# Causal masks of a four-layer transformer kernel moved wholly into PSUM, as 64x64 matmuls

## The chip, the cores and the metric

The kernel runs on one core of one Trainium2 chip. The metric is the device time of one execution in microseconds (us); three runs of the kernel before gave 1212.94 to 1221.29 us, median 1218.53.

## What is computed

Four layers, one after the other, on x of 4 sequences x 256 tokens x 512 features. Each layer normalises the rows, computes an attention s and a feed-forward g of the same normalised rows, and adds their product:

```python
xn = _layernorm(x, axis=-1)
s = _L0_attn_ref(xn, L0_attn_Wq, L0_attn_Wk, L0_attn_Wv, L0_attn_Wo)
g = _silu(_L0_ffn_ref(xn, L0_ffn_w_gate, L0_ffn_w_up, L0_ffn_w_down))
x = x + s * g
```

The attention of layers 0, 2 and 3 has 32 query heads and 8 key heads of 16 features, rotary positions and a causal mask (a key behind the query gets no weight); that of layer 1 has 32 key heads and neither. The causal part:

```python
scores = jnp.einsum('bhqd,bhkd->bhqk', q, k)
causal = jnp.triu(jnp.ones((S, S), dtype=bool), k=1)
scores = jnp.where(causal[None, None], -jnp.inf, scores)
attn = jax.nn.softmax(scores / jnp.sqrt(jnp.float32(hd)), axis=-1)
```

The feed-forward parts differ (ternary octonion weights, 4-bit weights, block-scaled weights, low-rank weights); the change leaves them alone.

## The kernel before

**Units and groups.** A layer's attention is worked in 8 units (a sequence and one half of its heads, 16 query heads), each in 4 groups of 4 heads; two layers make a run (r = 0: layers 0 and 1; r = 1: layers 2 and 3) of 16 units and 64 groups, numbered G. Each engine has its own program, written out by hand, and all go through the same slots: `slot(r, G)` is one group's turn on each engine. Between the runs stand the feed-forward parts of layers 0 and 2 (ffn0, ffn2), at the end that of layer 3; layer 1's and parts of the others fill slots.

**Stacks.** To get close to fp32 from fast matmuls, each head's query and key are split into a high and a low part. The parts stand side by side in a stack of 64 columns: 48 (STACK) carry data, column 48 is the place for the row's maximum (the key side holds 1 there), and columns 49 to 63 are zero. `set_pads(l)` and `set_key_pads(l)` on GpSimd fill these columns, once ahead of layer 0 (in ffn0) and once ahead of layer 2 (in ffn2). TensorE turns the stacks (L829, L843), two heads at a time, so that heads lie in partitions 0 to 63 and 64 to 127; a matmul over 64 partitions then gives scores, and two such matmuls use the two halves of the array's rows.

**Two kinds of scores.** `scores_rows` (L863; queries in partitions) serves only to find each query's maximum: VectorE reduces it (L1906), TensorE turns the maxima (L880), and SP copies them by DMA into row 48 of the turned queries (`place_maxima`). `scores_cols` (L905 for the causal layers; keys in partitions) computes the scores again with the maximum already subtracted, for two blocks of keys: kb = 1 (128 queries) and kb = 0 (256 queries). ScalarE takes the exponential of each (L1446) into `probs`, and `weigh_values` (L925) multiplies them with the values, four heads at once in four column tiles of the array (128*32), one slot later.

**The mask before.** For the row scores TensorE adds it in PSUM: for each of the two query blocks qb, four bf16 matmuls of 64 rows by 128 columns (L872), `cut_rows` against `cut_keys`. For the probabilities GpSimd sets the future to zero with `affine_select` (`cut_future`, L2139), two per group, at the head of its slot and ahead of the rest of its queue (`context_low`, `stack_low`, `scale_context`); `weigh_values` waits for them on `causal_cut`.

**The order of TensorE's slot.** `scores_cols(kb=1)` of group G; `scores_rows` qb = 0 and qb = 1 of group G + LEAD (five ahead); `scores_cols(kb=0)` of G; then, by slot, the turning of stacks, a projection (L812), parts of a feed-forward (L679, L712), the weighing of values of G - 1, an output projection (L950). The last five slots of layer 0 compute row scores of layer 1, which have no mask, and the last five of layer 3 none. The row scores of the first five groups of layers 0 and 2 are issued in ffn0 and ffn2, where a block of them stands between matmuls over the whole array.

**Constants.** SP loads 8 constants (CONSTS); VectorE copies the two of the mask into bf16 at step e = 2 of ffn0.

## Time and profile before

| what | value |
|---|---|
| three runs, median | 1218.53 us (1212.94 to 1221.29) |
| the profiled execution, its own time | 1219.86 us |
| its span, first to last instruction | 1218.1 us |
| mean granted TensorE clock | 0.986 of full speed |
| TensorE (PE) / its weight loads (PEld) | 94% / 69% of the span |
| VectorE (DVE) / ScalarE (ACT) / GpSimd (POOL) | 63% / 54% / 41% |
| causal slots, layer 0 | about 169 to 340 us |
| causal slots, layers 2 and 3 | about 835 to 1157 us |

Times in the trace are us from the start of the span. Matmuls are pipelined: a row's length reaches to its modelled end and overlaps the next, so the pace of TensorE is read from start to start. "64\*128" behind an operation is the part of the array that it uses, contraction rows by output columns; "128x512" is partitions by elements. A bracket at the end is the idle time ahead of it and what ended it; "issue" means that nothing the profile shows was waited for.

### The profile page before, as it was taken

To read this page: it belongs to the slowest core of one execution; us is meant where nothing else is said; L and a number is where in the kernel's file an instruction comes from. 1 tells how busy PE (TensorE), PEld (TensorE's weight loads), DVE (VectorE), ACT (ScalarE), POOL (GpSimd) and SP (SyncE) were. 2 spreads that over 40 slices of the span, in tenths; PEclk is the share of its full clock that TensorE was granted. 3 is DMA by queue.
4 is the path that set the end of the run, shared out by engine and by line. 5 is a ranking of instruction groups with operands and counts; after the bars stand their busy time and mean duration, and the time that the engine had idled before them with its cause. 6 is when DMAs were issued, how large, how long until landed. Compare 5 with 4: busy or idle time off the path is not lost.

```text
span 1218.1 us, 22076 instructions
## 1 busy us (share of the span) xinstructions
PE 1144.7 (94%) x8476; PEld 843.3 (69%) x8476; DVE 772.1 (63%) x1124; ACT 655.0 (54%) x1199; POOL 502.0 (41%) x648
## 2 busy tenths in 40 slices
PE   5999999999999999989999999999899999998997
PEld 4788876776656565556687888777677767676665
DVE  7843457785865746684644465545788777775545
ACT  4434347675555655564332333325867676776654
POOL 0000026564422212124555544432775566646552
PEclk8999989999999999999999999999999999999999
DMA  7000010030000100001243222210100101010001
GB/s 277 1 1 1 1 36 2 2 116 2 2 1 2 40 1 1 27 28 53 78 132 102 91 91 78 78 61 5 51 3 2 44 2 34 5 40 12 2 2 69
DMA packets 15258, 48.04 MB, mean 39 GB/s; under 512 B 2858, under 2 KB 6959, under 8 KB 14388
## 3 DMA queue, kind: packets, MB, share of 16 engines
q1 hardware_dynamic: 15156, 46.63, 11.4%
q8 instruction: 70, 1.15, 0.4%
q14 instruction: 32, 0.26, 0.1%
HBM read 44.00 MB, written 2.10 MB: 38 GB/s over the span
## 4 chain that ended last, share of the span: by engine, by line
PE 74%; DVE 12%; ACT 7%; issue 4%; DMA 2%; POOL 1%; DVEq 0%; ACTq 0%; SPq 0%; POOLq 0%
PE bank L679 18%; PE bank L812 16%; PE bank L712 9%; PE bank L950 8%; PE bank L925 6%; PE bank L863 4%; DVE negmax L1906 4%; PE bank L905 4%; ACT probs L1446 3%; DMA W_lo_whole<-in_w 2%; PE bank L872 2%; PE bank L829 1%; PE bank L630 1%; DVE W_lo_whole L1676 1%; ACT qT L1418 1%
## 5 line engine op out<-in xcount | busy, mean ns | idle before, releaser
L1906 DVE TENSOR_REDUCE negmax<-bank 128x4 f32<-128x1024 f32 (+1 forms) x256 | 250.5, 1017 | 100.1 <-PE bank L872 80.2
L1446 ACT ACTIVATE probs<-bank 128x512 f32<-128x512 f32 (+1 forms) x224 | 188.2, 847 | 52.4 <-PE bank L905 51.0
L2139 POOL TENSOR_SCALAR_AFFINE_SELECT probs<-probs 128x512 f32<-128x512 f32 x192 | 123.3, 648 | 169.1 <-ACT probs L1446 167.7
L2061 POOL TENSOR_TENSOR W_lo<-W_lo_whole,W_hi 128x512 fp32r<-128x512 f32 x84 | 117.3, 1425 | 100.0 <-ACT W_hi L1175 100.0
L925 PE MATMUL bank<-probs,V 128*32 128x256 f32 (+1 forms) x2048 | 117.3, 347 | 8.2 <-ACT probs L1446 4.5
L1175 ACT ACTIVATE W_hi<-W_lo_whole 128x1536 fp32r<-128x1536 f32 x28 | 41.7, 1489 | 130.7 <-DVE W_lo_whole L1676 130.7
L863 PE MATMUL bank<-kT,qT 64*128 64x256 f32 (+1 forms) x1024 | 102.6, 296 | 9.7 <-DVE xT_lo L1557 3.5
L905 PE MATMUL bank<-qT,kT 64*128 64x256 f32 (+1 forms) x512 | 97.2, 395 | 11.0 <-ACT qT L1418 4.1
L1457 ACT ACTIVATE pv<-bank 128x256 f32<-128x256 f32 x128 | 49.8, 389 | 97.7 <-PE bank L925 97.7
L925 PEld LDWEIGHTS bank<-probs,V 128*32 128x32 f32 x2048 | 53.6, 109 | 63.9 <-issue 28.5
L863 PEld LDWEIGHTS bank<-kT,qT 64*128 64x128 f32 x1024 | 79.0, 188 | 22.8 <-issue 7.7
L679 PE MATMUL bank<-xT_hi,W_hi 128*128 128x512 f32 x224 | 90.3, 403 | 4.1 <-ACT silu L1188 2.7
L812 PE MATMUL bank<-Wqkv,xT_whole 128*128 128x512 f32 (+1 forms) x256 | 87.9, 497 | 0.9
L1200 ACT ACTIVATE h_hi<-h_lo_whole 128x512 fp32r<-128x512 f32 x72 | 45.5, 633 | 80.2 <-DVE h_lo_whole L1688 52.2
L679 PE MATMUL bank<-xT_hi,W_lo 128*128 128x512 f32 x224 | 87.6, 391 | 0.0
L679 PE MATMUL bank<-xT_lo,W_hi 128*128 128x512 f32 x224 | 87.5, 391 | 0.0
L812 PEld LDWEIGHTS bank<-Wqkv,xT_whole 128*128 128x128 f32 x256 | 47.8, 192 | 38.0 <-issue 35.0
L1676 DVE TENSOR_TENSOR W_lo_whole<-W_lo_whole,block_scales 128x1536 f32<-128x1536 f32 x28 | 50.3, 1796 | 35.4 <-DMA W_lo_whole<-in_w 35.4
L1418 ACT ACTIVATE qT<-bank 128x512 fp32r<-128x512 f32 x128 | 69.4, 601 | 4.9 <-PE bank L829 4.9
L812 PE MATMUL bank<-Wqkv_hi,xT_hi 128*128 128x384 f32 x192 | 69.5, 362 | 2.6 <-ACT probs L1446 1.9
L905 PEld LDWEIGHTS bank<-qT,kT 64*128 64x128 f32 x512 | 48.1, 189 | 32.6 <-issue 23.3
L2108 POOL TENSOR_TENSOR scaled<-pvT,recip 128x256 f32<-128x256 f32 x64 | 43.1, 673 | 63.4 <-DVE recip L1937 63.4
(214 smaller groups left out, 2668.1 us busy)
## 6 DMA issues: line engine op xcount, KB each, us to landing
W_lo_whole<-in_w SPq DMA_DIRECT2D x28, 768.0 KB, 4.2
Wqkv_lo_whole<-in_Wqkv SPq DMA_DIRECT2D x6, 768.0 KB, 6.9
Wo_lo_whole<-in_Wo SPq DMA_DIRECT2D x4, 1024.0 KB, 5.3
Wqkv<-in_Wqkv SPq DMA_DIRECT2D x2, 1536.0 KB, 7.9
Wdown_whole<-in_Wd SPq DMA_DIRECT2D x1, 2816.0 KB, 14.6
x<-in_x SPq DMA_DIRECT2D x4, 512.0 KB, 6.4
out<-x SPq DMA_DIRECT2D x8, 256.0 KB, 2.0
V_lo_whole<-in_V SPq DMA_DIRECT2D x1, 1408.0 KB, 6.2
```

The costliest lines, as they stand in the source:

```text
L679: ins = mm(ps[:], lh, rh, start=(c == 0), stop=(c == len(terms) - 1))
L712: ins = mm(B.tensor(key), lh, rh, start=(j == 0 and c == 0), stop=(j == C - 1 and c == len(terms) - 1))
L812: ins = mm(ps[:, 0:width], lh, rh, start=(c == 0), stop=(c == len(terms) - 1))
L863: ins = mm(ps[:, par, pl * nk:(pl + 1) * nk], A[l].qT[u % 2][half, 2 * g + pl, qb * P:(qb + 1) * P], A[l].kT[u % 2][half, key_slot(l, g, p ...
L905: ins = mm(ps[:, par, pairs[0] * nq:pairs[1] * nq].rearrange("p (h q) -> p h q", h=n), A[l].kT[u % 2][r, key_slot(l, g, pairs[0]), kb * P: ...
L925: ins = mm(ps[32 * i:32 * i + 32, q0:SEQ], A[l].Vflat[u % 4][:, (kb * A[l].vh + kv) * CELL:(kb * A[l].vh + kv) * CELL + 32], A[l].probs[gi ...
L950: ins = mm(ps[:], lh, rh, start=(c == 0), stop=(c == len(terms) - 1))
L1418: nc.scalar.activation(A[l].qT[u % 2][:, 4 * half:4 * half + 4, tau * P:(tau + 1) * P], B.tensor(key).rearrange("p (a t) -> p a t", a=4), ...
L1446: nc.scalar.activation(A[l].probs[gi % 2][kb][:, :, q0 - kb * A[l].probs1:].rearrange("p (b h) q -> p b h q", b=2), B.tensor(key)[:, :, 0: ...
L1906: v.tensor_reduce(A[l].negmax[u % 2][:, qb, :].rearrange("p (b h) -> p b h", b=2)[:, :, 2 * g:2 * g + 2], B.tensor(key)[:, :, 0:2 * nk].re ...
L2061: ins = gp.tensor_tensor(lo, whole, hi.bitcast(F32), ALU.subtract)
L2139: gp.affine_select(out=blk, in_=blk, compare_op=ALU.is_ge, fill=0.0, base=0, pattern=[[0, 4], [1, P]], channel_multiplier=-1).then_inc(cau ...
```

## The change

- In the key stacks, one of the zero columns holds −2^100 for the keys in the second half (64 to 127) of a 128-token block, and in the query stacks the same column holds 1 for the queries in the first half; there is one such column per block (49 for the first, 50 for the second). The score matmuls of both kinds so add −2^100 to a whole 64x64 block of each diagonal 128x128 block, with no instruction of its own. `set_pads` writes these columns: 7 more instructions each for layers 0 and 2.
- What is left of the mask are the triangles of the two 64x64 blocks on the diagonal. For the row scores there are four matmuls per block as before, now of 64 rows by 64 columns, with the output on 64 partitions.
- The column scores get the same: four matmuls of 64 rows by 64 columns behind each of kb = 1 and kb = 0, ahead of the exponential.
- `cut_future` on GpSimd and the semaphore `causal_cut` are gone; `weigh_values` waits for the exponential of kb = 0.
- `cut_rows` and `cut_keys` become one constant `cuts` (128 x 5 x 64) and a second, `half_marks` (128 x 2). NEG is −2^100 instead of −1e30. GpSimd waits for the constants ahead of `set_pads(0)`.

```diff
--- before.py
+++ after.py
@@ -50,7 +50,7 @@
 STACK = 3 * SPLIT
 CELL = HD + 4
 RING = 6
-NEG = -1.0e30
+NEG = -2.0 ** 100
 ROUND = 1.5 * 2.0 ** 23
 WIDTH0 = 1366 // 8
 HID0, HC0 = 8 * WIDTH0, 11
@@ -269,8 +269,8 @@
         xn = [nc.alloc_sbuf_tensor_at(f"xn{i}", [P, D], F32, offset=names["gate"][0] + i * D * 4) for i in range(TILES)]
         ident = place("ident", [P, P], F32)
         ident_r = place("ident_r", [P, P], F32R)
-        cut_rows = place("cut_rows", [P, 2, P], BF16)
-        cut_keys = place("cut_keys", [P, 2, 2, 64], BF16)
+        cuts = place("cuts", [P, 5, 64], BF16)
+        half_marks = place("half_marks", [P, 2], F32)
         cosT = {l: place(f"cos{l}", [P, 2, HD], F32) for l in (0, 2, 3)}
         sinT = {l: place(f"sin{l}", [P, 2, HD], F32) for l in (0, 2, 3)}
         stats = place("stats", [P, TILES, 6], F32)
@@ -405,8 +405,7 @@
         assert at[0] <= R + first["V"] and R + first["negmax"] <= hidden_from
         at = [WP]
         ones = place("ones", [P, P], F32, at)
-        cut_rows_f = place("cut_rows_f", [P, 2, P], F32, at)
-        cut_keys_f = place("cut_keys_f", [P, 2, 2, 64], F32, at)
+        cuts_f = place("cuts_f", [P, 5, 64], F32, at)
         sign_in = place("sign_in", [P, KC, OCT], F32, at)
         sign_hid = place("sign_hid", [P, HC0, OCT], F32, at)
         compact0 = [nc.alloc_sbuf_tensor_at(f"compact{m}", [P, OCT, WIDTH0], F32, offset=WA + m * QKV_BYTES // 2)
@@ -515,7 +514,7 @@
             return Mark(nc, ctx, name, per_layer)
 
         ones_set = mark("ones_set", [3, 0, 0, 0])
-        mask_set = mark("mask_set", [3, 0, 0, 0])
+        mask_set = mark("mask_set", [2, 0, 0, 0])
         ln_stat = mark("row_stats", [TILES] * 4)
         ln_mom = mark("row_moments", [TILES] * 4)
         ln_var = mark("row_variance", [SEQS] * 4)
@@ -563,9 +562,8 @@
         HI = 2
         stack_hi = mark("stack_hi", [16 * HI] * 4)
         stack_lo = mark("stack_lo", [32] * 4)
-        PADS = [6 + 4 * 4, 4, 6 + 3 * 4, 0]
+        PADS = [6 + 7 + 4 * 4, 4, 6 + 7 + 3 * 4, 0]
         pads = mark("pads_set", PADS)
-        causal_cut = mark("causal_cut", [64, 0, 64, 64])
         rs_ready = mark("reciprocal_ready", [4 * SEQS] * 4)
         x_done = mark("x_updated", [TILES] * 4)
 
@@ -792,7 +790,7 @@
                     else:
                         pe.wait_ge(qkv_in[l][u], 16)
                 if u == 0 and tau == 0:
-                    pe.wait_ge(*mask_set.at(0, 3))
+                    pe.wait_ge(*mask_set.at(0, 2))
                 pe.wait_ge(*B.emptied(("xT", l, t)))
                 for key, c0, width in ([(("qkv", l, u, tau), 0, 384)] if GQA[l] else
                                        [(("qkv", l, u, tau), 0, 512), (("v", l, u, tau), 512, 256)]):
@@ -867,9 +865,9 @@
                     for j in range(2):
                         for par in range(2):
                             half = slice(64 * par, 64 * par + 64)
+                            dst = ps[64 * j:64 * j + 64, par, 0:2 * nk].rearrange("p (h k) -> p h k", h=2)
                             k0 = nk - P + 64 * j
-                            dst = ps[:, par, 0:2 * nk].rearrange("p (h k) -> p h k", h=2)[:, :, k0:k0 + 64]
-                            ins = mm(dst, cut_rows[half, j, :], cut_keys[half, j, :, :], start=False, stop=(j == 1))
+                            ins = mm(dst[:, :, k0:k0 + 64], cuts[half, 0, :], cuts[half, 1:3, :], start=False, stop=True)
                 ins.then_inc(B.fills(key), 1)
 
             def turn_max(l, u, bank=None):
@@ -904,7 +902,13 @@
                         r = slice(64 * par, 64 * par + 64)
                         ins = mm(ps[:, par, pairs[0] * nq:pairs[1] * nq].rearrange("p (h q) -> p h q", h=n),
                                  A[l].kT[u % 2][r, key_slot(l, g, pairs[0]), kb * P:(kb + 1) * P],
-                                 A[l].qT[u % 2][r, 2 * g + pairs[0]:2 * g + pairs[1], q0:SEQ], start=True, stop=True)
+                                 A[l].qT[u % 2][r, 2 * g + pairs[0]:2 * g + pairs[1], q0:SEQ], start=True, stop=not CAUSAL[l])
+                if CAUSAL[l]:
+                    for j in range(2):
+                        for par in range(2):
+                            r = slice(64 * par, 64 * par + 64)
+                            dst = ps[64 * j:64 * j + 64, par, 0:2 * nq].rearrange("p (h q) -> p h q", h=2)
+                            ins = mm(dst[:, :, 64 * j:64 * j + 64], cuts[r, 0, :], cuts[r, 3:5, :], start=False, stop=True)
                 ins.then_inc(B.fills(key), 1)
 
             def weigh_values(r, G, slot):
@@ -912,10 +916,7 @@
                 u, g = divmod(gi, GROUPS)
                 key = ("PV", l, gi)
                 ps = claim(key, values_bank(*divmod(slot, GROUPS)))
-                if CAUSAL[l]:
-                    pe.wait_ge(*causal_cut.at(l, 2 * (gi + 1)))
-                else:
-                    pe.wait_ge(*B.emptied(("ST", l, u, g, 0)))
+                pe.wait_ge(*B.emptied(("ST", l, u, g, 0)))
                 for tau in range(2):
                     pe.wait_ge(*B.emptied(("qkv" if GQA[l] else "v", l, u, tau)))
                 for kb in range(2):
@@ -1766,8 +1767,7 @@
                         scale_rows(0, LATE_ROWS[e + 1][0] // 2)
                     if e == 2:
                         dve.wait_ge(const_in, 16 * CONSTS)
-                        v.tensor_copy(cut_rows[:], cut_rows_f[:]).then_inc(mask_set.sem, 1)
-                        v.tensor_copy(cut_keys[:], cut_keys_f[:]).then_inc(mask_set.sem, 1)
+                        v.tensor_copy(cuts[:], cuts_f[:]).then_inc(mask_set.sem, 1)
                     if e + 2 < HC0 + LAG[0]:
                         ternary(after_step[e + 1], after_step[e + 2])
                     hidden(0, e)
@@ -2084,13 +2084,26 @@
 
             def set_key_pads(l):
                 for i in range(2):
-                    gp.memset(A[l].kstack[i][:, :, :, STACK:STACK + 1].bitcast(F32), 1.0).then_inc(pads.sem, 1)
-                    gp.memset(A[l].kstack[i][:, :, :, STACK + 1:64].bitcast(F32), 0.0).then_inc(pads.sem, 1)
+                    kr = A[l].kstack[i][:].rearrange("p n h s -> p (n h) s")
+                    ks = kr.bitcast(F32)
+                    gp.memset(ks[:, :, STACK:STACK + 1], 1.0).then_inc(pads.sem, 1)
+                    c = STACK + 1
+                    if CAUSAL[l]:
+                        if i == 1:
+                            gp.memset(ks[:, :, c:c + 1], 0.0).then_inc(pads.sem, 1)
+                        c += i
+                        gp.tensor_copy(kr[:, :, c], half_marks[:, 1:2].to_broadcast([P, 2 * A[l].kn])).then_inc(pads.sem, 1)
+                        c += 1
+                    gp.memset(ks[:, :, c:64], 0.0).then_inc(pads.sem, 1)
 
             def set_pads(l):
 
                 for i in range(2):
-                    gp.memset(A[l].qstack[i][:, :, STACK:64].bitcast(F32), 0.0).then_inc(pads.sem, 1)
+                    qs = A[l].qstack[i][:].bitcast(F32)
+                    c = STACK + 1 + i
+                    gp.memset(qs[:, :, STACK:c], 0.0).then_inc(pads.sem, 1)
+                    gp.tensor_copy(A[l].qstack[i][:, :, c], half_marks[:, 0:1].to_broadcast([P, UH])).then_inc(pads.sem, 1)
+                    gp.memset(qs[:, :, c + 1:64], 0.0).then_inc(pads.sem, 1)
                 set_key_pads(l)
                 for i in range(4):
                     gp.memset(A[l + 1].V[i][:, :, :, HD:HD + 1], 1.0).then_inc(pads.sem, 1)
@@ -2129,21 +2142,8 @@
                 gp.tensor_tensor(ks[:, :, 32:48], src[:, UH:UH + n, :], ks.bitcast(F32)[:, :, 0:16],
                                  ALU.subtract).then_inc(stack_lo.sem, 1)
 
-            def cut_future(r, G):
-                l, gi = group(r, G)
-                u, g = divmod(gi, GROUPS)
-                for kb in (1, 0):
-                    pool.wait_ge(*B.emptied(("ST", l, u, g, kb)))
-                    q0 = kb * (P - A[l].probs1)
-                    blk = A[l].probs[gi % 2][kb][:, :, q0:q0 + P]
-                    gp.affine_select(out=blk, in_=blk, compare_op=ALU.is_ge, fill=0.0, base=0,
-                                     pattern=[[0, 4], [1, P]], channel_multiplier=-1).then_inc(causal_cut.sem, 1)
-
             def slot(r, G):
                 U, g = divmod(G, GROUPS)
-                l, u = unit(r, U)
-                if CAUSAL[l]:
-                    cut_future(r, G)
                 if pair_turned(G - 1) is not None:
                     context_low(r, pair_turned(G - 1))
                 if r == 0 and (U, g) == (6, 0):
@@ -2216,6 +2216,7 @@
             for b in range(2, SEQS):
                 inverse_deviation(0, b)
             pool.wait_ge(*B.filled(("up", 0, 1, 4)))
+            pool.wait_ge(const_in, 16 * CONSTS)
             set_pads(0)
             for u in range(2):
                 for tau in range(2):
@@ -2246,7 +2247,7 @@
                 load(x[:, 2 * b:2 * b + 2, :], xv[:, 2 * b:2 * b + 2, :], x_in[b])
             load(W0_whole[2][:], a["Wd0"], ffn_in[2])
             n = 0
-            for dst, name in [(cut_rows_f, "cut_rows"), (cut_keys_f, "cut_keys")] + [(cosT[l], f"cos{l}") for l in (0, 2, 3)] + \
+            for dst, name in [(cuts_f, "cuts"), (half_marks, "half_marks")] + [(cosT[l], f"cos{l}") for l in (0, 2, 3)] + \
                     [(sinT[l], f"sin{l}") for l in (0, 2, 3)]:
                 load(dst[:], a[name], const_in)
                 n += 1
@@ -2356,15 +2357,13 @@
     eye = np.eye(P, dtype=np.float32)
     o["ident"] = eye
     r = np.arange(64)
-    rows = np.zeros((64, 2, P), np.float32)
-    rows[r, 0, r] = 1
-    rows[r[:63], 1, 64 + r[:63]] = 1
-    rows[63, 1, 0:64] = 1
-    keys = np.zeros((64, 2, 2, 64), np.float32)
-    keys[:] = np.where(r[None, :] > r[:, None], np.float32(NEG), np.float32(0))[:, None, None, :]
-    keys[63, 1] = NEG
-    o["cut_rows"] = np.concatenate([rows, rows])
-    o["cut_keys"] = np.concatenate([keys, keys])
+    cuts = np.zeros((64, 5, 64), np.float32)
+    cuts[r, 0, r] = 1
+    cuts[:, 1:3] = np.where(r[None, :] > r[:, None], np.float32(NEG), np.float32(0))[:, None, :]
+    cuts[:, 3:5] = np.where(r[None, :] < r[:, None], np.float32(NEG), np.float32(0))[:, None, :]
+    second = np.arange(P) >= 64
+    o["half_marks"] = np.stack([np.where(second, 0.0, 1.0), np.where(second, NEG, 0.0)], 1).astype(np.float32)
+    o["cuts"] = np.concatenate([cuts, cuts])
     which, sign = octonion_table()
     i_of = np.arange(D) // 64
     o["sign_in"] = np.ascontiguousarray(sign[i_of].reshape(KC, P, OCT).transpose(1, 0, 2))
```

## Rows read from the trace of the kernel before

**Rows 1.** The page: busy time by engine.

```profile
PE 1144.7 (94%) x8476; PEld 843.3 (69%) x8476; DVE 772.1 (63%) x1124; ACT 655.0 (54%) x1199; POOL 502.0 (41%) x648
```

**Rows 2.** Stretches: length, then busy of PE, PEld, DVE, ACT, POOL; granted clock.

```profile
170.00:330.00 160.00, 154.01 (x1478) 110.26 (x1482) 115.42 (x180) 106.08 (x214) 88.64 (x134) 0.97 0.07 24
...
815.00:1000.00 185.00, 173.71 (x1773) 132.94 (x1772) 134.91 (x214) 125.56 (x260) 103.98 (x148) 0.99 0.07 23
1000.00:1165.00 165.00, 153.81 (x1495) 111.30 (x1494) 112.12 (x176) 115.39 (x226) 102.63 (x138) 0.99 0.05 17
```

**Rows 3.** The page: shares of the chain that ended last, by engine.

```profile
PE 74%; DVE 12%; ACT 7%; issue 4%; DMA 2%; POOL 1%; DVEq 0%; ACTq 0%; SPq 0%; POOLq 0%
```

**Rows 4.** TensorE groups by form: busy, mean ns | idle before, its releaser.

```profile
L925 PE MATMUL bank<-probs,V 128*32 128x256 f32 x1280 | 96.2, 391 | 8.2 <-ACT probs L1446 4.5 <-DVE negmax L1906 3.5
...
L872 PE MATMUL bank<-cut_keys,cut_rows 64*128 64x128 bf16 x768 | 57.8, 224 | 0.0
```

**Rows 5.** Timeline, one causal slot, rows of TensorE: start, length, operation.

```profile
207.81 0.39 PE L905 MATMUL bank<-qT,kT 64*128 64x256 f32 x2
208.02 0.35 PE L863 MATMUL bank<-kT,qT 64*128 64x128 f32 x4
208.19 0.30 PE L872 MATMUL bank<-cut_keys,cut_rows 64*128 64x128 bf16 x4
208.29 0.49 PE L863 MATMUL bank<-kT,qT 64*128 64x256 f32 x4
208.61 0.30 PE L872 MATMUL bank<-cut_keys,cut_rows 64*128 64x128 bf16 x4
208.71 0.49 PE L905 MATMUL bank<-qT,kT 64*128 64x512 f32 x2
```

**Rows 6.** Same timeline: weight loads, GpSimd select, next weighing of values.

```profile
205.97 0.64 POOL L2139 TENSOR_SCALAR_AFFINE_SELECT probs<-probs 128x512 f32<-128x512 f32 x1 [0.77 <-ACT probs L1446]
...
208.19 0.13 PEld L872 LDWEIGHTS bank<-cut_keys,cut_rows 64*128 64x128 bf16 x4
...
210.38 0.86 PE L925 MATMUL bank<-probs,V 128*32 128x256 f32 x16 [0.18 <-ACT probs L1446]
```

**Rows 7.** Timeline of TensorE: row scores between whole-array matmuls.

```profile
787.19 0.44 PE L863 MATMUL bank<-kT,qT 64*128 64x128 f32 x4
787.47 0.29 PE L872 MATMUL bank<-cut_keys,cut_rows 64*128 64x128 bf16 x4
...
790.32 0.39 PE L679 MATMUL bank<-xT_hi,W_lo 128*128 128x512 f32 x1
790.63 0.50 PE L863 MATMUL bank<-kT,qT 64*128 64x256 f32 x4
790.98 0.28 PE L872 MATMUL bank<-cut_keys,cut_rows 64*128 64x128 bf16 x4
791.19 0.50 PE L712 MATMUL bank<-W_hi,h_hi 128*128 128x512 f32 x1
```

**Rows 8.** Timeline of TensorE: two groups of one array shape, a bank wait between.

```profile
147.97 0.39 PE L679 MATMUL bank<-xT_lo,Wup 128*128 128x512 f32 x1
148.20 0.39 PE L712 MATMUL bank<-Wdown,h_hi 128*128 128x512 f32 x1
```

**Rows 9.** Timeline: from whole-array matmuls to four column tiles.

```profile
206.56 0.33 PE L812 MATMUL bank<-Wqkv_lo,xT_hi 128*128 128x384 f32 x1
...
206.74 0.34 PE L812 MATMUL bank<-Wqkv_hi,xT_lo 128*128 128x384 f32 x1
207.00 0.16 PEld L925 LDWEIGHTS bank<-probs,V 128*32 128x32 f32 x8 [0.25 <-issue]
```

**Rows 10.** Engines and granted clock (PEclk) in a stretch behind waits.

```profile
170.00:180.00 10.00, 9.08 (x51) 7.80 (x52) 5.46 (x8) 5.28 (x11) 4.79 (x8) 0.51 0.01 2
```

**Rows 11.** Timeline of GpSimd around set_pads(2).

```profile
634.45 0.12 POOL L2098 MEMSET V<- 128x32 f32 x1
638.01 4.24 POOL L2061 TENSOR_TENSOR W_lo<-W_lo_whole,W_hi 128x512 fp32r<-128x512 f32 x3 [3.44 <-ACT W_hi L1175]
```

## What the change does to the time: the prediction

> **What bounds the kernel now.** I read the busy times first. TensorE is busy for 94% of the span; VectorE follows with 63% and GpSimd, which does the work that is taken away, has 41% [rows 1]. Three stretches hold nearly all slots of the causal layers. In them TensorE is busy for 154.01 of 160, 173.71 of 185 and 153.81 of 165 us, so idle for 5.99 + 11.29 + 11.19 = 28.5 us in all, while GpSimd stands still for 45, 44 and 38% of them [rows 2]. The chain that ended last agrees: 74% of it is TensorE and 1% GpSimd [rows 3]. So the question is what the change does to TensorE's sequence. Can GpSimd's part bring anything? TensorE's wait ahead of the weighing of values (L925) is 8.2 us in the whole kernel, and neither releaser named is GpSimd [rows 4]. One instance shows why: the select of a group starts at 205.97 and takes 0.64, so it ends at 206.61, and the matmuls that need it start at 210.38 [rows 6], 3.8 us later. The 0.18 us of idle there is called "<-ACT" although that work was long done. The gate by GpSimd is hidden.
>
> **The price of a change of array shape.** The key is in TensorE's timeline. The page prints the shape that a matmul takes of the array: 128\*128, 64\*128 for scores (two at once, one in each half of the rows), 128\*32 for the weighing. Inside one shape a new group costs nothing: L679 to L712 is 0.23 us with a bank wait between, the step of 512 columns [rows 8], which makes 0.055 for 128 columns and 0.11 for 256. At a change of shape it does cost:
> - In: the last 512-column matmul starts at 790.32 and the first 64\*128 at 790.63, 0.31 instead of 0.23: 0.08.
> - First loads, which nothing hides now: the block of four 128-column scores lasts 0.28 (787.19 to 787.47) against 0.17 (208.02 to 208.19) behind its own shape: 0.11. With 256 columns it lasts 0.35 (790.63 to 790.98) against 0.32 (208.29 to 208.61), 0.03.
> - Out: the mask block is 0.10 when its own shape follows (208.61 to 208.71), and 0.21 when a whole-array matmul follows (790.98 to 791.19): 0.11 [rows 5, 7].
> A change of columns alone behaves so too: from 128\*128 to 128\*32 the step is 0.26 instead of 0.18, again 0.08, and the weight loads stand still for 0.25 [rows 9]. The mask matmuls are 64\*128 today, so the run of scores in a slot is all one shape: columns kb1, rows qb0, mask, rows qb1, mask, columns kb0. The new ones take 64 rows by 64 columns, a fourth shape, and stand four times in that run. The trace has no 64\*64. The Trainium skill (TensorEngine Tiling (Array Packing), Key Properties) says in so many words that "Changing tiling mode (not just tile) drains the TensorE", and its list has 64×64 as a mode beside 64×128. By that rule each mask block pays in and out, which raises the chance of my forecast; the trace agrees at every other change of shape, with about 0.2 us in and out.
>
> **The change part by part.** All sums are against the profiled execution, 1219.86 us (span 1218.1 and 1.8 around it).
> - A mask block of 64\*64. In: 0.08. The four run at once if they use separate quarters, as the two halves do today (four matmuls in 0.10, two turns of 0.05): 0.05. Their loads are now open: the four of today take 0.13 together [rows 6], with half the columns 0.06. Out: 0.11. Sum 0.30. Bounds of one block: 0.05 if no shape change is paid; 0.08 + 0.13 + 0.10 + 0.11 = 0.42 if nothing shrinks with the columns.
> - A slot of a causal layer that also has row scores of one. Four blocks: 1.20. The scores behind them load openly: rows qb0 0.11, rows qb1 0.03, columns kb0 0.11: 0.25. Off: two mask blocks of today at 0.10, 0.20; columns kb1 to rows qb0, which takes 0.21 today for 0.11 of columns because of the loads, 0.10 [rows 5]; the last way out, which the slot pays today as well, 0.11. Sum 1.20 + 0.25 − 0.20 − 0.10 − 0.11 = 1.04 us. There are 96 causal slots; the last 5 of layer 0 and the last 5 of layer 3 have no causal rows (those run five groups ahead). 86 × 1.04 = 89.4.
> - Those 10 slots, two column masks only: 2 × 0.30 + 0.11 − 0.10 − 0.11 = 0.50 each: 5.0.
> - The 20 row blocks issued among the FFN matmuls of layers 0 and 2: 14 are followed by another shape anyway (0.30 − 0.11 − 0.10 = 0.09), 6 are not (0.30 + 0.03 − 0.10 = 0.23): 2.6.
> - The whole blocks through the stacks cost TensorE nothing: the marks sit in padding columns that the 64-row matmuls read already. GpSimd gets 7 more small fills and copies in each of set_pads(0) and set_pads(2). The fills are 0.12 us each there; behind set_pads(2), which ends at 634.57, GpSimd waits 3.44 us for its next work [rows 11]. Were every one as dear as the 0.64 of the select [rows 6], it would be 4.5, 1 us too late at most; I take 0. VectorE copies one constant fewer, SP issues the same 8 loads with fewer bytes: 0.
> - Removed from GpSimd: 192 selects. The wait on causal_cut becomes one on the exponentials, which were done 0.6 us earlier still. What is queued behind the selects on GpSimd (context_low, stack_low, scale_context) comes earlier, and the chain has 1% of GpSimd: 0, and it is at most a share of the 28.5 us of idle.
> - The exponentials of both column blocks start later, by the new mask. ScalarE is busy for 66 to 70% of these stretches and VectorE for 68 to 73% [rows 2], so both have room, and a slower TensorE shortens waits on them. Where TensorE waits now for ScalarE's qT, that chain starts behind the scores of the same slot and moves along with them, so I take back only a quarter of the 28.5 us: −7.
> Sum: 89.4 + 5.0 + 2.6 − 7 = +90 us. 1219.86 + 90 = 1309.9; the profiled execution stands 1.3 us above the median of 1218.53, so 1309 us, 7.4% slower. About 1% is what a measurement of this kernel can tell from no change.
>
> **Rivals.**
> - No price for 64\*64 after 64\*128 (not slower by what can be told). The way: the row split stays two, and only the column split changes; the array goes on as inside one shape. For: no row shows this pair of shapes, and nothing in the code asks for a change beyond the size. Against: the column split alone cost 0.08 at 206.74 to 207.00 [rows 9]. Then the 192 new column blocks cost 0.05 to 0.10 each, 9.6 to 19, and the 192 row blocks fall from 0.10 to 0.05 or stay, −9.6 to 0, and up to 7 come back: between −7 and +19, middle +8: 1227. It decides as long as the way into and out of a block costs under 0.02 us together (384 blocks × 0.02 = 8).
> - GpSimd was the brake (faster). The selects stand in front of stack_low and context_low in GpSimd's queue; without them the stacks come earlier, and every idle moment of TensorE in these stretches goes: −28.5, with +8 for the masks −20: 1198. It needs the rival above and releases that the chain (1% GpSimd) doesn't show.
> - The four quarters don't run together (the change doesn't do what it is built for). Each mask block streams 4 × 0.055 = 0.22 instead of 0.05: +0.17 × 384 = +65, with my +90: 1374.
> - The clock falls more often. TensorE's granted clock was 0.51 in 170 to 180, behind waits [rows 10], where its busy time was 9.08 of 10, and 0.97 or more over each whole stretch [rows 2]. Such a stretch loses about half its work, 5 us; four more of them would make 1329.
>
> **How the numbers follow.** My forecast has 0.70, no price for the shape 0.18, GpSimd as the brake 0.05, quarters one by one or a falling clock 0.07. The likeliest case has its own range: the low end leaves out all open loads (per slot 1.04 − 0.25 − 4 × 0.06, and the 0.10 behind columns kb1 is not saved: 0.65) and gives back all 28.5 us, 96 × 0.65 + 2.6 − 28.5 = +36: 1255. The high end takes 0.42 for a block and gives nothing back, 97 + 384 × 0.12 = +143: 1362. The range of 8 in 10 leaves out the last third of that, where every block would have to be at its dearest, and reaches down toward the first rival: 1235 to 1340. Slower by over 1%: 0.70 + 0.07 + a third of 0.18 = 0.83; within 1%: 0.12; faster: 0.05.
>
> **What would show it.** Right: a row of 64\*64 matmuls whose next group starts about 0.2 us later rather than 0.05 to 0.10; a causal slot's run from columns kb1 to the end of columns kb0 about 1 us longer; 86 × 7 + 10 × 3 + 14 + 6 × 2 = 658 more changes of shape, with the weight loads standing still for "issue" at them; the FFN stretches unchanged; GpSimd's busy time down by 192 × 0.64 = 123 us with no effect. Wrong: if the rows behind a 64\*64 block start within 0.06 us of its last turn, the price of the shape was wrong and the first rival holds; if the exponentials or the reductions grow idle ahead of TensorE, the bound has moved.

## The result, and the profile after

The changed kernel takes 1285.01 us (four runs, 1283.41 to 1287.27) beside 1215.84 (four runs) for the kernel before on the same chip: 1.0558 times [1.053, 1.0587], some 68 us more. The profiled execution has a span of 1281.6 us against 1218.1, so 63.5 more, at a granted clock of 0.991 (0.986 before).

The page of the kernel after, busy times and then the chain by engine; the rows of before are [rows 1] and [rows 3]:

```profile
PE 1220.1 (95%) x9244; PEld 873.4 (68%) x9244; DVE 760.2 (59%) x1123; ACT 658.7 (51%) x1199; POOL 379.2 (30%) x470
...
PE 79%; DVE 10%; ACT 6%; issue 3%; DMA 2%; POOL 0%; ACTq 0%; SPq 0%; DVEq 0%; POOLq 0%
```

TensorE got 768 matmuls and 75 us of busy time more, GpSimd 123 us less, and the chain moved further onto TensorE. Where do the 63.5 us lie? I cut both spans at the same matmuls: the causal slots of layer 0, and those of layers 2 and 3. Before (columns: PE, PEld, DVE, ACT, POOL busy, granted clock, DMA share, GB/s):

```profile
169.00:344.80 175.80, 168.94 (x1594) 119.91 (x1594) 126.89 (x198) 112.86 (x225) 94.98 (x142) 0.97 0.07 22
...
835.00:1155.00 320.00, 298.76 (x3094) 222.08 (x3096) 234.53 (x368) 226.54 (x459) 200.15 (x276) 0.99 0.06 19
```

After:

```profile
170.60:365.90 195.30, 190.77 (x1850) 128.47 (x1850) 123.86 (x198) 113.57 (x225) 54.44 (x78) 0.99 0.06 20
...
855.80:1218.80 363.00, 350.14 (x3604) 243.81 (x3604) 225.18 (x368) 229.58 (x459) 118.35 (x150) 0.99 0.05 17
```

What lies between the two, layer 1 (344.8 to 571.7, then 365.9 to 593.0: 226.9 and 227.1) and the feed-forward of layer 2 (263.3 and 262.8), stays as it was. The causal slots grow by 19.5 and by 43.0: 62.5 of the 63.5. The granted clock rose a little in them, so it isn't the clock.

TensorE's timeline of one slot of after, from columns kb1 to the first turning of a stack; its like of before is in [rows 5]:

```profile
212.18 0.39 PE L903 MATMUL bank<-qT,kT 64*128 64x256 f32 x2
212.49 0.25 PE L911 MATMUL bank<-cuts 64*64 64x128 bf16 x4
212.67 0.44 PE L861 MATMUL bank<-kT,qT 64*128 64x128 f32 x4
213.04 0.25 PE L870 MATMUL bank<-cuts 64*64 64x128 bf16 x4
213.22 0.51 PE L861 MATMUL bank<-kT,qT 64*128 64x256 f32 x4
213.66 0.25 PE L870 MATMUL bank<-cuts 64*64 64x128 bf16 x4
213.84 0.50 PE L903 MATMUL bank<-qT,kT 64*128 64x512 f32 x2
214.27 0.25 PE L911 MATMUL bank<-cuts 64*64 64x128 bf16 x4
214.45 0.88 PE L827 MATMUL bank<-ident_r,qstack 128*128 128x128 f32 x8
```

Read it from start to start. A mask block holds the next group off by 0.18 each time (212.49 to 212.67), where 0.10 was the whole of it inside one shape. The groups of scores between the blocks are longer too: 0.31, 0.37, 0.44 and 0.43, since each pays the way out to the block and opens with loads that nothing hides. The run takes 2.27 us, where an undisturbed one of before takes 1.32. Called "run" below: the time from the start of columns kb1 to the start of the first group of another shape.

### The profile page after: what moved, and what is told of

It is laid out like the page before. It is cut to its first block, busy times and chain, and to the rows that moved or that the text cites. A ratio compares the mean times of both kernels' runs of the same rounds, so it can differ in the third digit from the quotient of the medians.

```text
span 1281.6 us, 23433 instructions
## 1 busy us (share of the span) xinstructions
PE 1220.1 (95%) x9244; PEld 873.4 (68%) x9244; DVE 760.2 (59%) x1123; ACT 658.7 (51%) x1199; POOL 379.2 (30%) x470
## 4 chain that ended last, share of the span: by engine, by line
PE 79%; DVE 10%; ACT 6%; issue 3%; DMA 2%; POOL 0%; ACTq 0%; SPq 0%; DVEq 0%; POOLq 0%
PE bank L677 17%; PE bank L810 16%; PE bank L710 8%; PE bank L951 8%; PE bank L861 7%; PE bank L926 6%; PE bank L903 6%; PE bank L911 3%; PE bank L870 3%; ACT probs L1447 3%; DVE negmax L1906 2%; DMA W_lo_whole<-in_w 1%; PE bank L827 1%; PE bank L628 1%; DVE W_lo_whole L1677 1%
## 5 line engine op out<-in xcount | busy, mean ns | idle before, releaser
L1906 DVE TENSOR_REDUCE negmax<-bank 128x4 f32<-128x1024 f32 (+1 forms) x256 | 252.0, 1022 | 148.4 <-PE bank L870 127.5
L1447 ACT ACTIVATE probs<-bank 128x512 f32<-128x512 f32 (+1 forms) x224 | 189.5, 846 | 118.7 <-PE bank L911 113.7
L861 PE MATMUL bank<-kT,qT 64*128 64x256 f32 (+1 forms) x1024 | 114.2, 310 | 7.0 <-DVE negmax L1906 1.7
L861 PEld LDWEIGHTS bank<-kT,qT 64*128 64x128 f32 x1024 | 75.6, 186 | 26.8 <-issue 5.0
L2138 POOL TENSOR_TENSOR qstack<-rope_cos,qstack 128x256 fp32r<-128x256 f32 x48 | 36.6, 763 | 192.7 <-ACT kstack L1412 192.7
L1201 ACT ACTIVATE h_hi<-h_lo_whole 128x512 fp32r<-128x512 f32 x72 | 45.4, 630 | 80.8 <-DVE h_lo_whole L1689 52.4
L2129 POOL TENSOR_TENSOR ctxT_lo<-ctxT_lo_whole,ctxT_hi 128x256 fp32r<-128x256 f32 x48 | 36.7, 764 | 153.3 <-ACT ctxT_hi L1464 153.2
```

Of the source, the lines that this page charges most:

```text
L861: ins = mm(ps[:, par, pl * nk:(pl + 1) * nk], A[l].qT[u % 2][half, 2 * g + pl, qb * P:(qb + 1) * P], A[l].kT[u % 2][half, key_slot(l, g, p ...
L1447: nc.scalar.activation(A[l].probs[gi % 2][kb][:, :, q0 - kb * A[l].probs1:].rearrange("p (b h) q -> p b h q", b=2), B.tensor(key)[:, :, 0: ...
L1906: v.tensor_reduce(A[l].negmax[u % 2][:, qb, :].rearrange("p (b h) -> p b h", b=2)[:, :, 2 * g:2 * g + 2], B.tensor(key)[:, :, 0:2 * nk].re ...
```

## The experiments

All runs stand against the kernel before on the same chip; "run" is the median over the causal slots of layer 0 / of layers 2 and 3, waits inside it and ahead of the next group included. Most of the small differences below are under 1%; one is called a difference where its interval leaves out 1.

| kernel | time / before [95%] | run, us |
|---|---|---|
| before | 1 | 1.33 / 1.42 |
| after | 1.0558 [1.053, 1.0587] | 2.27 / 2.27 |
| wide | 1.0124 [1.0088, 1.0159] | 1.64 / 1.64 |
| late | 1.0517 [1.0476, 1.0559] | 2.20 / 2.24 |
| paired | 1.0335 [1.0304, 1.0365] | 1.88 / 1.90 |
| rows_only | 1.0221 [1.0185, 1.0257] | 1.71 / 1.72 |
| cols_only | 1.0282 [1.0241, 1.0322] | 1.88 / 1.88 |
| no_select | 0.9958 [0.9937, 0.9979] | 1.33 / 1.42 |
| free_rows | 0.9929 [0.9908, 0.995] | 1.23 / 1.24 |
| no_triangles | 0.9846 [0.9825, 0.9867] | 1.23 / 1.24 |
| wide_free | 0.9964 [0.9946, 0.9982] | 1.36 / 1.36 |
| select_last | 0.9965 [0.9945, 0.9985] | 1.23 / 1.24 |

### Shape or number? The same masks as 64 rows by 128 columns (wide)

The stationary side becomes the identity beside 64 columns of zeros, so a mask matmul fills 128 output partitions and stays in the shape of the scores. Number of matmuls, order, waits and GpSimd are those of after.

```diff
-dst = ps[64 * j:64 * j + 64, par, 0:2 * nk]...
-ins = mm(dst[...], cuts[half, 0, :], cuts[half, 1:3, :], start=False, stop=True)
+dst = ps[:, par, 0:2 * nk]...
+ins = mm(dst[...], cuts[half, 1 - j:3 - j, :]..., cuts[half, 3:5, :], start=False, stop=(j == 1))
```

> The changed kernel with the same eight mask matmuls more per slot, but each of 64 rows by 128 columns (an identity beside zeros as the stationary operand), so that the array keeps the 64*128 shape of the scores around it. Theory (the price is the change of array shape): a mask block costs 0.10 us as in the kernel before; a slot's run from columns kb1 to the end of columns kb0 is 1.32 + 0.20 = 1.52 us instead of 2.27, in all 19 us of work more than before, of which waits inside the run take back some 8: about 1228 us. Rival (768 matmuls more, whatever their shape, and the exponentials that wait for them): about as slow as the changed kernel, 1285 us.

Measured: 1.0124, 1234.83 us. The slot of wide:

```profile
211.44 0.38 PE L903 MATMUL bank<-qT,kT 64*128 64x256 f32 x2 [0.21 <-ACT qT L1419]
211.63 0.31 PE L911 MATMUL bank<-cuts 64*128 64x128 bf16 x4
211.82 0.44 PE L861 MATMUL bank<-kT,qT 64*128 64x128 f32 x4
212.07 0.31 PE L870 MATMUL bank<-cuts 64*128 64x128 bf16 x4
212.17 0.50 PE L861 MATMUL bank<-kT,qT 64*128 64x256 f32 x4
212.50 0.31 PE L870 MATMUL bank<-cuts 64*128 64x128 bf16 x4
212.60 0.50 PE L903 MATMUL bank<-qT,kT 64*128 64x512 f32 x2
212.94 0.29 PE L911 MATMUL bank<-cuts 64*128 64x128 bf16 x4
213.18 0.43 PE L810 MATMUL bank<-Wqkv_hi,xT_hi 128*128 128x384 f32 x1
```

With as many matmuls, each of more columns, the two inner row blocks hold the next group off by 0.10, not 0.18, and the groups ahead of them shrink to 0.25 and 0.33. So the number isn't the main cost: of after's 5.6%, 4.3 points belong to the shape. What is left, 1.2, is the price of two further blocks at all, less what the missing selects give back. That price was put too low: the run is 1.64 and not the expected 1.52, and the kernel 1234.83 us and not 1228. The two new blocks hold their followers off by more than 0.10: the one behind columns kb1 by 0.19 (211.63 to 211.82), the one behind columns kb0, with a whole-array matmul next, by 0.24.

### One kind of triangle at a time (rows_only, cols_only)

rows_only takes the column triangles out and puts GpSimd's selects back; it has not one matmul more than before, only a smaller shape for the row masks. cols_only is after with the row masks in the wide form.

```diff
 # rows_only
-dst = ps[64 * j:64 * j + 64, par, 0:2 * nq]...          # in scores_cols
-ins = mm(dst[...], cuts[r, 0, :], cuts[r, 3:5, :], start=False, stop=True)
+cut_future(r, G)                                        # GpSimd's slot
 # cols_only
-ins = mm(dst[...], cuts[half, 0, :], cuts[half, 1:3, :], start=False, stop=True)
+ins = mm(ps[:, ...], cuts[half, 1 - j:3 - j, :]..., cuts[half, 3:5, :], start=False, stop=(j == 1))
```

> The changed kernel with 64*64 triangles for the row scores only; the probabilities are cut by GpSimd as before. As many matmuls as before. Theory: two of the four changes of shape in a slot: run 1.69 instead of 1.32 us, +32 us of work and 3 in the FFN parts, 10 to 15 taken back by waits inside the run: about 1238 us. Rival (number of matmuls): 1216 us, no change.

> The changed kernel with 64*64 triangles for the column scores, and 64*128 ones for the row scores as in the kernel before; no GpSimd select. Theory: run 1.89 instead of 1.32 us, 55 us of work more, some 15 taken back: about 1256 us, and with rows_only the two add up to the whole change. Rival (number of matmuls): all of the change, 1285 us.

Measured: 1.0221 (1245.83 us) and 1.0282 (1254.18 us). rows_only lies 8 us above the expected 1238, of which some 5 are the chip (before takes 1220.67 there, 1215.84 where the expectations started from). The slot of rows_only:

```profile
211.19 0.39 PE L904 MATMUL bank<-qT,kT 64*128 64x256 f32 x2
211.40 0.35 PE L862 MATMUL bank<-kT,qT 64*128 64x128 f32 x4
211.68 0.25 PE L871 MATMUL bank<-cuts 64*64 64x128 bf16 x4
211.86 0.51 PE L862 MATMUL bank<-kT,qT 64*128 64x256 f32 x4
212.29 0.25 PE L871 MATMUL bank<-cuts 64*64 64x128 bf16 x4
212.47 0.50 PE L904 MATMUL bank<-qT,kT 64*128 64x512 f32 x2
212.91 0.89 PE L828 MATMUL bank<-ident_r,qstack 128*128 128x128 f32 x8
```

This is the cleanest of the set: the same 8 mask matmuls, with half the columns, and 2.2% more time. The run grows from 1.32 to 1.71, 0.20 for each of the two excursions into 64\*64 in place of a block in the scores' own shape. cols_only confirms it from the other end: after's run of 2.27 falls to 1.88 when its two row blocks go back to 64\*128, again 0.20 each, and its time is the 1256 us expected within 2. The ratios of the two add up to 5.0 of the 5.6%. The Trainium skill (TensorEngine Tiling (Array Packing), Key Properties) says that a change of tiling mode drains TensorE. The trace agrees that the changes cost time and gives the price, 0.20 us for the way in and back; a drain as such can't be seen in it.

### Fewer excursions with the same matmuls (late, paired)

late collects the four mask blocks and issues them behind columns kb0: one excursion. paired issues the first three ahead of columns kb0, which keeps its own: two.

```diff
-scores_cols(l, u, g, 1)
-scores_rows(r, G + LEAD, 0)
-scores_rows(r, G + LEAD, 1)
-scores_cols(l, u, g, 0)
+later = []
+scores_cols(l, u, g, 1, later)
+scores_rows(r, G + LEAD, 0, None, later)
+scores_rows(r, G + LEAD, 1, None, later)
+scores_cols(l, u, g, 0, later)          # late; paired: one line lower, without later
+for triangles in later:
+    triangles()
```

> The changed kernel with its 64*64 mask matmuls all moved behind the scores of columns kb0 in the slot, four blocks in a row: one way into the shape and the way out that is paid anyway, instead of four of each. The exponential of kb1 and the reductions start later for it, by up to 1 us. Theory: run of about 1.12 + 0.08 + 4 x 0.09 = 1.56 us, 23 us of work more than before, some of it taken back: about 1231 us, up to 1245 if the later exponential is felt. Rival (number of matmuls, and the wait of the exponentials for them): 1285 us or more.

Measured: 1.0517, 1281.37 us, nearly as slow as after. One slot of late, from columns kb0 on:

```profile
1042.81 0.49 PE L910 MATMUL bank<-qT,kT 64*128 64x512 f32 x2
1043.24 0.25 PE L918 MATMUL bank<-cuts 64*64 64x128 bf16 x4
1043.32 0.28 PE L870 MATMUL bank<-cuts 64*64 64x128 bf16 x8
1043.43 0.23 PE L918 MATMUL bank<-cuts 64*64 64x128 bf16 x4
1044.34 0.41 PE L810 MATMUL bank<-Wqkv_hi,xT_hi 128*128 128x384 f32 x1 [0.69 <-ACT probs L1464]
```

The excursions did go: the four blocks start within 0.19 us. But the next group now waits 0.69 for the exponential of kb1, whose bank it takes, and that exponential can only begin once its triangles are in. The waits of late in layers 2 and 3 show it (total, times, longest):

```profile
PE bank L827 <- ACT probs L1464: 19.8, 29, 0.7
...
PE bank L810 <- ACT probs L1464: 17.6, 26, 0.7
```

55 waits of 0.7, 37.4 us, and 32 more in layer 0 (22.2 us). The expectation had allowed for a late exponential, but with 1245 us at most. So late moved the cost into a wait. Without it the commonest run, 2.11, would be 1.42, less than the 1.56 expected; the time of the kernel alone doesn't show this. paired was made to part the two:

> As late, but the mask blocks of columns kb1 and of both row scores stand in a row ahead of columns kb0, and that of kb0 behind it: two ways into the 64*64 shape in a slot instead of four, the same matmuls, and the exponential of kb1 frees its bank in time for the work behind the run. Theory (price of the change of shape): run of about 1.72 us against 2.27 of the changed kernel and 1.32 of the one before; with what the waits take back about 1243 us, halfway between them. Rival (number of matmuls): 1285 us as the changed kernel. If late was slow for another reason than its late exponential of kb1 (found: 0.7 us of idle behind the masks, ended by that exponential), this one is as slow as late, 1281.

Measured: 1.0335, 1257.89 us. Its slot:

```profile
1024.03 0.25 PE L918 MATMUL bank<-cuts 64*64 64x128 bf16 x4
1024.11 0.28 PE L870 MATMUL bank<-cuts 64*64 64x128 bf16 x8
1024.32 0.51 PE L910 MATMUL bank<-qT,kT 64*128 64x512 f32 x2
1024.75 0.25 PE L918 MATMUL bank<-cuts 64*64 64x128 bf16 x4
1025.26 0.41 PE L810 MATMUL bank<-Wqkv_hi,xT_hi 128*128 128x384 f32 x1 [0.25 <-ACT probs L1464]
```

Two excursions fewer than after, and the run falls from 2.27 to 1.88. I had expected 1.72 and 1243 us. The block of twelve lasts 0.29 (1024.03 to 1024.32), so the quarters are filled as fast as hoped. What is too long is the last step, and it is a wait again: the group behind the run needs the bank that the exponential of kb1 leaves. In the slot shown that is 0.25 of the 0.51 behind 1024.75; in the common slot the last step is 0.38 (1003.20 to 1003.58, with 0.13 idle) where after has 0.18. So 0.13 to 0.20 of the 1.88 is this wait, and without it two excursions fewer would have taken 0.52 to 0.59 off the run, 0.26 to 0.30 each. That is more than the 0.20 of rows_only because here a block isn't put back into the scores' shape, where its step is 0.10, but joined to another, where it adds 0.05 to 0.06 ((0.29 − 0.18) / 2), and because scores without a block between them hide their loads. The number of matmuls is that of after, and the time is 2.2 points less: the rival of the number is out.

### GpSimd's part alone (no_select), and TensorE's alone (no_triangles, free_rows)

no_select is before without the selects (the future isn't taken out of the probabilities). no_triangles is after without triangles on either kind of scores and without selects: only whole 64x64 blocks are masked. free_rows is that with the selects, so the whole of the attention is computed: the row scores give a maximum that may be that of a future key in the same 64x64 block, and a shift by it cancels in the normalisation.

```diff
 # no_select
-pe.wait_ge(*causal_cut.at(l, 2 * (gi + 1)))
+pe.wait_ge(*B.emptied(("ST", l, u, g, 0)))
-cut_future(r, G)
 # free_rows, against after (no_triangles: only the first two lines)
-ins = mm(dst[...], cuts[half, 0, :], cuts[half, 1:3, :], ...)
-ins = mm(dst[...], cuts[r, 0, :], cuts[r, 3:5, :], ...)
-pe.wait_ge(*B.emptied(("ST", l, u, g, 0)))
+pe.wait_ge(*causal_cut.at(l, 2 * (gi + 1)))
+cut_future(r, G)
```

> The kernel before without GpSimd's 192 selects: the causal cut of the probabilities is left out, and the weighing of values waits for the exponentials instead. Theory (the selects are hidden): no change, 1216 us within 3. Rival (the selects held up stack_low and context_low in GpSimd's queue): up to 20 us faster, 1196.

> No mask matmul and no GpSimd select: the triangles of the causal mask are left out for both kinds of scores, only the marks in the stacks remain. Theory: as free_rows within 3 us, about 1207, since GpSimd's part is hidden; against the changed kernel this is the whole price of the 64*64 blocks, about 78 us. Rival (GpSimd's queue matters once TensorE has less to do): 5 to 15 us below free_rows.

> No mask matmul at all: the row scores get only the marks in the stacks (whole 64x64 blocks), so that a query's maximum may come from a later key of its own 64-block, which softmax does not mind; the probabilities are cut by GpSimd's select as in the kernel before. Theory: two blocks of 0.10 us fewer in 86 slots, 17 us of work less and 2 in the FFN parts, of which growing waits inside the run keep half: about 1207 us. Rival (VectorE's reductions bound the row scores): 1216 us, no change.

Measured: 0.9958, 0.9846 and 0.9929. The first says that the selects are not wholly hidden: 0.4% of 1220 is 5 us, and between free_rows and no_triangles they are worth 1210.91 − 1200.87 = 10. So no_triangles went by its rival (5 to 15 us below free_rows) and not by my theory (within 3). The last says that the row triangles aren't needed at all: free_rows has the lowest median here of the kernels that compute everything, 0.7% below before. (The shift cancels as long as the future key's score isn't so far above the others that their exponentials vanish.)

Where do hidden selects cost anything? In VectorE's products for the rotary positions in layers 2 and 3 (mean ns behind the busy time). The first of the three groups, before:

```profile
L1890 DVE TENSOR_TENSOR rope_cos<-qk,cos 128x320 f32<-128x320 f32 x27 | 17.1, 634 | 0.0
```

And in no_select, three lines higher up:

```profile
L1887 DVE TENSOR_TENSOR rope_cos<-qk,cos 128x320 f32<-128x320 f32 x27 | 12.9, 477 | 0.0
```

634 ns fall to 477; the other two groups go from 600 to 548 and from 652 to 528. One instance of before shows the two side by side (VectorE and GpSimd in its timeline):

```profile
210.39 0.64 POOL L2139 TENSOR_SCALAR_AFFINE_SELECT probs<-probs 128x512 f32<-128x512 f32 x1 [0.26 <-ACT probs L1446]
210.63 0.74 DVE L1890 TENSOR_TENSOR rope_cos<-qk,cos 128x320 f32<-128x320 f32 x1
211.29 0.48 DVE L1893 TENSOR_TENSOR rope_sin<-qk,sin 128x320 f32<-128x320 f32 x1
```

The product that starts inside a select takes 0.74, the next, outside, 0.48. The Trainium skill (SBUF — State Buffer, SBUF: two separate sides) says why this could be: a VectorE operation with two operands in SBUF and a GpSimd operation that reads SBUF shut each other out. The trace agrees that the one is held up, though by 0.26 and not by the 0.40 that the select still had to run. The difference is the same throughout: in before 27 such products start inside a select with 0.3 us or more of it left, and each takes longer than 0.48 by the rest of the select less 0.13 to 0.14 (0.57 left, 0.44 lost). The 67 products with nothing on GpSimd beside them take 0.48 in the mean. This isn't peculiar to the select: 38 products that overlap only other operations of GpSimd take 0.81.

### Mask the columns cheaply, or move the selects (wide_free, select_last)

wide_free is wide without the row triangles: TensorE masks the columns in the scores' own shape, GpSimd nothing. select_last is free_rows with the selects at the end of GpSimd's slot, to tell the queue order from the contention.

```diff
 # wide_free, against wide
-ins = mm(dst[...], cuts[half, 1 - j:3 - j, :]..., cuts[half, 3:5, :], start=False, stop=(j == 1))
 # select_last, against free_rows
-cut_future(r, G)             # head of GpSimd's slot
 ...
 scale_context(r, pair_complete(G))
+cut_future(r, G)
```

> As wide (masks of the probabilities by 64*128 matmuls, no select on GpSimd), but without triangles for the row scores, as in free_rows. A slot has two mask blocks of 0.10 us, as many as the kernel before, and GpSimd no select. Theory: TensorE's work is that of the kernel before, and what GpSimd's selects took from VectorE is gone: as no_select, 1215 us, or a few below it. If the selects were wholly hidden: 1219.

> free_rows with GpSimd's selects moved behind context_low, stack_low and scale_context in its slot. no_triangles was 10 us faster than free_rows, with the selects as the only difference. If they cost by holding up that queue: 1203 us. If they cost by slowing VectorE's operations at the same time (its rope operations take 0.55 to 0.68 us with selects and 0.48 to 0.53 without): as free_rows, 1211 us, or slower where the select is now late for the weighing of values.

Measured: 0.9964 (1212.59 us) and 0.9965 (1212.05 us). Both lie below before with an interval that leaves out 1, and neither below free_rows, whose interval touches theirs. wide_free needs 1.36 for a run against 1.23: two mask blocks cost TensorE about what the missing selects give back. Behind the rest of its queue the select holds up nothing there, and still nothing is won (1203 us was expected if it were the queue, 1211 if it were VectorE), so GpSimd's order isn't what it costs. VectorE's rotary products are no shorter for it either: over the whole kernel they take 617 ns in the mean in free_rows and in select_last, 560 in no_triangles. That the contention with VectorE accounts for all of the 5 to 10 us is what is left over, not shown.

## Why the prediction was right, and where it wasn't

**Direction and mechanism held.** The forecast (0.70) said that each 64\*64 block is a change of shape and back, and that this alone makes the kernel slower. wide, rows_only and paired show it from three sides, and the time lies in the range. The trace of after has 659 changes of shape more than that of before (1133 against 474), where 658 were forecast. The bound was TensorE, as read: 62.5 of 63.5 us lie in the causal slots, and the rest of these stages, outside the runs, went only from 126.5 to 125.7 and from 222.3 to 221.0 us. The rival without a price for the shape needed less than 0.02 us a block, and it is 0.20.

**Where the 26 us too much came from.** The sum said +90, the profiled execution shows +63.5. About 17 of the difference lie in the −7, 8 in the price of a slot and 1.5 in the row blocks among the feed-forwards.

**The price.** Predicted for a slot: +1.04. A run without a wait grew from 1.32 to 2.27, +0.95. By starts: rows qb0 with the way in behind them were put at 0.17 + 0.11 + 0.08 = 0.36 and take 0.37, rows qb1 at 0.32 + 0.03 + 0.08 = 0.43 and take 0.44; the block itself at 0.05 + 0.06 + 0.11 = 0.22, and it takes 0.18. Two other parts were off and partly made up for each other. Columns kb1 came to 0.21 − 0.10 + 0.08 = 0.19 in the sum and take 0.31: the 0.10 that was to be saved behind them isn't. Columns kb0 came to 0.50 and take 0.43. So taking each part from another pair of shapes was good to a tenth for the slot as a whole, but that closeness is in part luck: 0.16 and 0.07 too much, 0.12 too little. The four quarters run together, as assumed: in paired the step of twelve mask matmuls is 0.29 us, where one after the other they would need 12 × 0.055 = 0.66. In after the row of the loads is

```profile
214.27 0.11 PEld L911 LDWEIGHTS bank<-cuts 64*64 64x64 bf16 x4 [0.24 <-issue]
```

0.11 for four, where I had put 0.06. So the rival with one quarter at a time is out, and the one with the falling clock too (0.991 over the span).

**The step that failed is the −7.** Runs without a wait would have grown by 86 × 0.95, and by 5 × 0.55 and 5 × 0.35 in the slots without row scores, 86 us in all; the stages grew by 62.5, so about 24 us were given back, not 7. I asked which waits outside the scores would shrink, and took a quarter of the idle time. But waits stand inside the runs, where my price, taken from a run without any, doesn't see them. A slot of before:

```profile
970.25 0.39 PE L905 MATMUL bank<-qT,kT 64*128 64x256 f32 x2
970.95 0.44 PE L863 MATMUL bank<-kT,qT 64*128 64x128 f32 x4 [0.32 <-DVE xT_lo L1557]
...
971.75 0.48 PE L905 MATMUL bank<-qT,kT 64*128 64x512 f32 x2
972.16 0.54 PE L829 MATMUL bank<-ident_r,qstack 128*128 128x128 f32 x4
```

1.91 us, not 1.32: columns kb1 are done and the bank of the row scores isn't free. Summed over a stage, the runs of before are 7.1 and 17.5 us longer than so many without a wait, those of after 3.4 us together: 21 us. In after the mask block stands just in this gap, and costs nothing as long as the wait would have been longer. Some 2.4 of the 21 are something else: the first two slots of layer 0, in before partly at half clock [rows 10], in after hardly (0.88 from 170 to 180). Another 2.1 went outside the runs. It isn't the missing selects that emptied the gaps: no_select still has nearly the excess of before (its runs are 3 us shorter in all), and rows_only, which keeps the selects, has 18 us left of before's 25. The size of the gift is thus shown by the sums; which wait gave how much wasn't tried by itself.

**GpSimd's part: 0 predicted, 5 to 10 us measured.** The wait that I looked at (L925) was hidden, as I said, and it stayed so; in after the weighing waits no less:

```profile
L926 PE MATMUL bank<-probs,V 128*32 128x256 f32 x1280 | 96.1, 390 | 8.8 <-ACT probs L1447 5.1 <-DVE negmax L1906 3.5
```

That is 8.8 where it was 8.2 [rows 4]. What I left out is that an engine with no one waiting for it can still slow another. The rival "GpSimd was the brake" was therefore not empty, but it holds 0.4%, not 2.

**The small terms.** The fills and copies of set_pads cost nothing, as put: behind those of set_pads(2) GpSimd still waits, now for 2.63 instead of 3.44 [rows 11], and behind those of set_pads(0) for 26.0 instead of 26.4.

```profile
655.97 0.12 POOL L2111 MEMSET V<- 128x32 f32 x1
658.72 4.25 POOL L2061 TENSOR_TENSOR W_lo<-W_lo_whole,W_hi 128x512 fp32r<-128x512 f32 x3 [2.63 <-ACT W_hi L1176]
```

The 20 row blocks among the feed-forwards were put at 2.6; ffn0 grew by 1.6 (169.0 to 170.6) and ffn2 shrank by 0.5. VectorE and ScalarE did become later and not the bound: VectorE waits 148.4 us ahead of its reductions (100.1 in before) and ScalarE 118.7 ahead of its exponentials (52.4),

```profile
L1906 DVE TENSOR_REDUCE negmax<-bank 128x4 f32<-128x1024 f32 (+1 forms) x256 | 252.0, 1022 | 148.4 <-PE bank L870 127.5
L1447 ACT ACTIVATE probs<-bank 128x512 f32<-128x512 f32 (+1 forms) x224 | 189.5, 846 | 118.7 <-PE bank L911 113.7
```

both of them mostly waiting for TensorE.

## What to carry to other kernels

Look at the shape a small matmul takes of the array and at that of its neighbours, not only at its size: smaller matmuls of another shape cost more than larger ones of the same, and if they can't be avoided they are collected in one place, unless a consumer waits for the first of them. When time is added to the bounding engine, look for its waits inside the very stretch that grows, since they take part of it up. And ask first whether the work is needed at all: the mask on scores that serve only for a maximum could go.

## What the runs showed that I had not expected

- A mask block of 64\*64 among scores of 64\*128 costs 0.20 us more than one of 64\*128 (rows_only against before, after against cols_only), 0.16 as the mean of after's four against wide's.
- A mask block of 64\*128 among scores of that shape costs the 0.10 of its step, but taking both out shortens the run only from 1.32 to 1.23. The rest goes into a wait for the exponential of kb1: free_rows has 0.15 idle in such a slot (1085.16 to 1085.72 behind columns kb0), and a run takes 1.14 where the next group doesn't wait for it (1090.48 to 1091.62). Where the next group takes its bank, that exponential is a floor under the run, in paired and late too.
- VectorE's products of 128x320 take 477 to 548 ns in the mean without GpSimd's selects and 600 to 652 with them (no_select and before, layers 2 and 3). One that starts inside a select loses the rest of it less 0.13 to 0.14 us.
- Moving 16 tiny matmuls behind one group (late) brought 60 us of waits for an exponential, about as much as late is slower than before.
